# Eight activation loads a turn issued by GpSimd's DMA queue in place of SP's, in a two-layer graph attention kernel

## What is computed

```python
# layer 0: 8 heads of 64, masked softmax attention
h = maximum(layernorm(x), 0.0)
q, k, v = h @ Wq + bq, h @ Wk + bk, h @ Wv + bv
weights = softmax(q @ k.T / sqrt(64) + mask(adj))      # per head
x = x + weights @ v
# layer 1: rel is normed by row, there is no softmax
h = maximum(layernorm(x), 0.0)
rel = adj.T * ((h @ Wq.T) @ (h @ Wk.T).T)
rel = rel / norm(rel, axis=2)
x = x + rel @ (h @ Wv.T)
```

## Time and profile before

| | |
|---|---|
| median of three runs | 2420.07 us |
| profiled execution, its own time | 2422.38 us |
| span of the profiled execution | 2420.6 us |
| granted TensorE clock over the span | 0.999 |
| PE busy | 2391.3 us, 99% |
| ScalarE busy | 1686.1 us, 70% |
| VectorE busy | 1454.1 us, 60% |
| GpSimd busy | 1301.7 us, 54%, 1159 instructions |
| DMA queue q1 (SP's), share of 16 engines | 63.3% |
| x_in loads, issue to landing | 3.1 us, 128 of 256 KB |
| x_res loads, issue to landing | 3.3 us, 124 of 256 KB |

### The profile page before, as it was taken

One profiled execution on the slowest core, in us unless ns is written; L12 is line 12 of the kernel. 1 busy time (PEld: TensorE's weight loads), 2 busy tenths in 40 slices (PEclk: granted clock), 3 DMA queues, 4 the chain that ended last, 5 costly groups with the idle time before them and its releaser, 6 DMA issues.

```text
span 2420.6 us, 53556 instructions
## 1 busy us (share of the span) xinstructions
PE 2391.3 (99%) x19252; PEld 1299.4 (54%) x19252; DVE 1454.1 (60%) x4435; ACT 1686.1 (70%) x4111; POOL 1301.7 (54%) x1159
## 2 busy tenths in 40 slices
PE   8999999999999999999999999999999999999998
PEld 4455555555555555555555555555555555555554
DVE  5665666655666555665556665556655566655664
ACT  5867777667776677776777766777667777667773
POOL 3655555555555555555555555555555555555561
PEclk9999999999999999999999999999999999999999
DMA  7756676666677566776566765667755667656663
GB/s 206 148 123 125 136 152 140 135 129 130 133 153 140 115 131 133 153 141 128 128 131 144 149 137 121 132 132 153 143 127 127 132 146 149 131 124 135 134 125 70
DMA packets 938361, 328.09 MB, mean 136 GB/s; under 512 B 886000, under 2 KB 886256, under 8 KB 938096
## 3 DMA queue, kind: packets, MB, share of 16 engines
q1 hardware_dynamic: 935312, 319.43, 63.3%
q10 hardware_dynamic: 2784, 5.24, 0.6%
HBM read 72.88 MB, written 33.55 MB: 44 GB/s over the span
## 4 chain that ended last, share of the span: by engine, by line
PE 90%; DMA 2%; ACT 2%; DVE 2%; issue 1%; POOL 1%; DVEq 0%; SPq 0%; ACTq 0%
PE B L728 76%; PE S L804 7%; PE O L728 7%; DMA probs_t<-halves 2%; ACT probs L529 1%; DVE stats L592 0%; ACT h L473 0%; ACT halves L537 0%; DVE masked L665 0%; POOL v L423 0%; DVE rel_halves L699 0%; POOL halves L427 0%; ACT h_halves L480 0%; DVE result L706 0%; DVE v_sum L657 0%
## 5 line engine op out<-in xcount | busy, mean ns | idle before, releaser
L427 POOL TENSOR_TENSOR halves<-probs,halves 128x512 f16<-128x512 f32 x512 | 598.1, 1168 | 561.5 <-ACT halves L537 561.2
L529 ACT ACTIVATE probs<-masked,neg_max 128x256 f32<-128x256 f32 x1024 | 508.3, 498 | 204.4 <-DVE neg_max L665 204.2
L665 DVE CUSTOM_DVE_ANT_0 masked<-S,mask 128x256 f32<-128x256 f32 x1024 | 385.7, 415 | 129.8 <-PE S L804 125.5
L413 POOL TENSOR_TENSOR h_halves<-h,h_halves 128x512 f16<-128x512 f32 x256 | 295.3, 1159 | 155.7 <-ACT h_halves L480 155.7
L728 PE MATMUL B<-wv,h0t 128*128 128x512 f16 x1536 | 354.1, 380 | 3.9 <-DMA h0t<-h_halves 2.5
L728 PE MATMUL B<-h0t,wq 128*128 128x512 f16 x1536 | 352.8, 379 | 0.0
L728 PE MATMUL B<-h0t,wk 128*128 128x512 f16 x1536 | 352.5, 379 | 0.0
L728 PE MATMUL B<-h1t,wm 128*128 128x512 f16 x1488 | 336.5, 379 | 1.3 <-DMA h1t<-h_halves 1.3
L728 PE MATMUL B<-wvt,h1t 128*128 128x512 f16 x1488 | 336.7, 379 | 1.1 <-issue 1.1
L537 ACT ACTIVATE halves<-probs 128x512 f16<-128x512 f32 x512 | 322.6, 630 | 20.3 <-PE O L728 4.2
L728 PEld LDWEIGHTS O<-v,probs_t 128*128 128x128 f16 x6144 | 245.8, 98 | 126.1 <-DMA probs_t<-halves 9.9
(11 more groups left out here) (78 smaller groups left out, 2983.0 us busy)
## 6 DMA issues: line engine op xcount, KB each, us to landing
x_in<-in_x_dram SPq DMA_DIRECT2D x128, 256.0 KB, 3.1
out_dram<-result SPq DMA_DIRECT2D x128, 256.0 KB, 3.4
x_res<-in_x_dram SPq DMA_DIRECT2D x124, 256.0 KB, 3.3
probs_t<-halves SPq DMA_TRANSPOSE x512, 2.8
h0t<-h_halves SPq DMA_TRANSPOSE x132, 3.2
h1t<-h_halves SPq DMA_TRANSPOSE x124, 3.3
rq<-in_L_gnn_Wq_dram ACTq DMA_DIRECT2D x4, 256.0 KB, 4.9
x_res<-in_L_gnn_Wk_dram ACTq DMA_DIRECT2D x4, 256.0 KB, 5.4
```

The source lines that it names most:

```text
L413: nc.gpsimd.tensor_tensor(h_halves[:, n, 1, :], h[:, n % 2, :], h_halves[:, n, 0, :], ALU.subtract).then_inc(h_low[layer], 1)
L427: nc.gpsimd.tensor_tensor(halves[:, n % RING, 1, :], probs[:, n % 2, :, :].rearrange("p t n -> p (t n)"), halves[:, n % RING, 0, :], ALU.s ...
L529: ins = nc.scalar.activation(probs[:, n % 2, i, :], masked[:, n % 2, i, :], ACT.Exp, bias=neg_max[:, n % 2, i:i + 1], scale=-1.0, accum_ou ...
L665: ins = nc.vector.tensor_tensor_reduce(out=masked[:, n % 2, i, :], in0=S[n % 4][:, i, :], in1=mask[:, i, :], scale=SCORE, scalar=BIG, op0= ...
```

## The change

The branches for x_in and x_res move from SP's walk through PLAN into GpSimd's, at the same places of the list and with the same waits. The first four loads of x (pair 0) and everything else stay with SP. Since the first x_in loads and the later ones now come from different queues, the later ones count on semaphores of their own (x_next), and the wait of VectorE's statistics is written for these. 124 loads of x_in and 124 of x_res move, 248 in all.

```diff
+        x_next = [sem(f"x_next{t}") for t in range(TILES)]
...
             for kind, n, p in PLAN:
-                if kind == "x_in" and p > 0:
-
-                    sp.wait_ge(ln_done[0], TILES * (p - 1) + n + 1)
-                    sp.dma_start(x_in[:, n, :], xv[p][:, n, :]).then_inc(x_loaded[n], 16)
-                elif kind == "x_res" and p < PAIRS - 1:
-
-                    if p == 0 and n == 0:
-                        sp.wait_ge(w_low, 6)
-                    if p == 1 and n == 0:
-                        sp.wait_ge(setup_product, KT)
-
-                    need(sp, r_done, R_COUNT.get(("out", n, p - 2), 0))
-                    sp.dma_start(x_res[:, p % 2, n, :], xv[p][:, n, :]).then_inc(res_loaded[p % 2], 16)
-                elif kind == "split":
+                if kind == "split":
...
             for kind, n, p in PLAN:
-                if kind == "v":
+                if kind == "x_in" and p > 0:
+
+                    pool.wait_ge(ln_done[0], TILES * (p - 1) + n + 1)
+                    pool.dma_start(x_in[:, n, :], xv[p][:, n, :]).then_inc(x_next[n], 16)
+                elif kind == "x_res" and p < PAIRS - 1:
+
+                    if p == 0 and n == 0:
+                        pool.wait_ge(w_low, 6)
+                    if p == 1 and n == 0:
+                        pool.wait_ge(setup_product, KT)
+
+                    need(pool, r_done, R_COUNT.get(("out", n, p - 2), 0))
+                    pool.dma_start(x_res[:, p % 2, n, :], xv[p][:, n, :]).then_inc(res_loaded[p % 2], 16)
+                elif kind == "v":
...
-                    dve.wait_ge(x_loaded[n], 16 * (p + 1))
+                    dve.wait_ge(x_next[n], 16 * p)
```

## The result

The changed kernel takes 2452.1 us (median of four runs, 2451.3 to 2458.3), the kernel before on the same chip 2420.4 (2419.9 to 2421.0): a ratio of 1.0135, interval 1.0123 to 1.0147. That is 31.7 us more; the forecast was 39.6 more, range 2430 to 2495.

The account below looks back on a forecast made before the run. TensorE was taken to bound every undisturbed turn. Delays of 0.80 + 0.52 = 1.32 us a turn over 30 turns gave 39.6 us, added to 2420.1: 2459.7, said as 2460 us, range 2430 to 2495.

Parts of the forecast that it names:

- The bound and the chain: TensorE bounds every undisturbed turn; one chain without slack from GpSimd's sq_pow to VectorE's q_st delays it, 1.32 us a turn.
- The sq_pow wait for data: Sign at GpSimd's sq_pow: this wait gone, and VectorE's wait for sq_pow up by 0.8 us in one of two cases.
- the wait of the statistics for the residual: Sign on VectorE: its statistics' wait for GpSimd's residual goes up from 1.2 to about 2.5 us.
- D: Time one load issue holds GpSimd, taken as 1.01 us, bounded by 0.43 and 1.80.
- the row of guess: Profile row of GpSimd's own instruction on four elements a partition, 1.01 us, used to price a load issue.
- the formula: Delay of q_st, and TensorE with it, once a turn: 2D - 0.70 us, over 30 turns.
- the sum: Delays ahead of sq_pow (0.80 us) and unit 1's low half (0.52): 1.32 us a turn, 30 turns, 39.6 us.
- The rival of dearer issues: GpSimd and VectorE hold each other up, so an issue takes 1.8 us or more: 2507 us; chance 0.11.
- the lower bound of 0.43: Least time SP takes to issue the same load, 0.43 us; on GpSimd it would give a 5 us loss.
- Landing: x_res loads behind unit 5's low half land about when they did; priced at 0, at most 0.5 us a turn.
- the faster rival: Loads gone from SP's queue ahead of transposes; half of TensorE's 14.1 us waiting for probs_t goes: 2413 us; chance 0.06.

## Why the prediction was right, and where it was not

**The bound and the chain: right.** TensorE bounds each turn, there was nothing to win, and the loss came in at q_st by the two x_in loads. The sq_pow wait for data is gone (37.3 us in 33 times before, 31.0 in 4 now), the wait of the statistics for the residual is 1.57 us in the turn shown (1.25 before; forecast 2.5), and the undisturbed turn lost 0.46 us (forecast 1.32).

**The size of D: the term that was mis-sized.** I took 1.01 us from the row of guess and set aside SP's median of 0.577, which would have been right to a hundredth: GpSimd took 0.57. Here the same instruction on another engine was the nearer row, and not another kind of instruction on the same engine. With D = 0.57 the formula gives 30 x 0.44 = 13 us and a forecast of 2433.

**The formula: right in sum, partly by accident.** 2D - 0.70 = 0.44 to 0.46, and 0.46 was measured. But comparing the starts of the chain's steps with the kernel before (medians over the turns), 0.33 us is lost at sq_pow, 0.01 around unit 1's low half and v, and 0.13 along VectorE's ln_work beside the x_res load behind unit 3 (0.10 of it in the operation that took 0.27), a place that the sum did not have. The rival of dearer issues had named this contention, in both directions, but had priced it as an issue of 1.8 us or more. What came was VectorE held up by a tenth of a microsecond, with the issue as short as ever. The formula also holds only from D = 0.49 on, since a gap can't be filled by less than nothing: at the lower bound of 0.43 it should have given 30 x 0.22 = 6.6 us and not 5, and the loss ends at D = 0.21, not 0.35.

**Landing: the step that failed.** I priced it at 0, at most 0.5 us a turn, because I asked only for whom the loads land, and compared their own flight. The loads themselves land 0.5 to 0.7 us later (x_in after 3.6 us, 3.1 before; x_res after 4.0, 3.3 before), and the residual's wait for them grew by 3 us in the whole run: so far the step was right. What I did not ask is what flies beside them. SP's order had kept these loads behind unit 5's transpose; on another ring they leave at the same moment and their packets are first. That is about 14 us in the turns of the profiled execution; by the run that only occupies GpSimd it is an estimated 19 of the 31.7 us. In the faster rival I even took the loads' absence from SP's ring for a gain of up to 7 us. There was nothing to gain: with no load between units 0 and 1 and all on SP the time is that of before, and on GpSimd's ring there is a loss.

So the forecast of 39.6 was near to 31.7 by luck: one term too large by a factor of three (39.6 for some 13) stood beside one that was missing (14 to 19).

**What stays open.** Why unit 1 waits 7 to 11 us in the four runs with x_res on GpSimd and the x_in load between units 0 and 1 on SP, and only 2.2 in the changed kernel: in the packets of one such turn the load, two stores and the transpose are mingled for 6 us, but which of the three decides it was not separated. Unit 2 shows the same pattern: 7.2 us to landing with two x_res loads by GpSimd beside it and SP's x_in load between units 0 and 1, and 5.2 without the latter. And the disturbed turns don't make up all of the difference of medians everywhere: e.g. 6.5 us with SP's loads ahead, of which the trace of its fastest run shows none.

## What to carry to other kernels

Moving a transfer to another queue changes more than who issues it: it gives up the order that the one ring kept. List the transfers that were queued ahead of it, and ask for each of them how much slack its reader has should the moved one arrive first. For the price of an issue on another engine, the same instruction's row on the engine it comes from was the right one here. And where the move is wanted, the places decide: the same eight loads cost 31.7 us or 5.9.

## What the runs showed of the hardware

The queues' rows of the changed kernel:

```profile
q1 hardware_dynamic: 899600, 254.40, 54.0%
q0 software_dynamic: 19840, 65.03, 11.1%
```

A load of 256 KB is 80 packets in GpSimd's ring (19840 / 248) and was 144 in SP's (q1 had 935312 before): by size 64 of 4096 bytes against 128 of 2048, and 16 of 4 bytes in both. The large ones take 159 ns each, the smaller 84 (medians). The first ones of a load take far longer, 0.7 to 1.2 us for the first nine in the turn shown. A transpose's packets, of 256 bytes, take 18 ns.

From the start of an x_in load's issue to its first packet it is 1.28 us by GpSimd and 1.21 by SP (medians of 120). The Trainium skill (DMA: Bandwidth & Descriptors, Specifications) has 1 us against 0.6; these traces don't show that difference.

VectorE's TENSOR_SCALAR on four elements, begun 0.3 us into GpSimd's load issue or its memset, ends with them (0.27 and 0.29 us for 0.17), while the TENSOR_TENSOR just ahead of it, beside the same instruction, keeps its 0.16. By the Trainium skill (SBUF — State Buffer, SBUF: two separate sides) the port pair that the two engines share is locked for a whole instruction; it matters to a VectorE operation in a 2-port mode, and to one with two SBUF inputs only if GpSimd's instruction reads SBUF.
